# First attention of a four-layer megakernel: Wv and Wo folded per head, weights applied to the normalised tokens, context transposed by the host

## The reference

```
xn = layer_norm(x, gamma_x, beta_x)            # the 64 context tokens of ctx_1024
ln = layer_norm(latents, gamma_l, beta_l)      # the 64 tokens of x
q = ln @ Wq                                    # 8 heads of 64
k_x, v_x = split(xn @ Wkv);  k_l, v_l = split(ln @ Wkv)
k_x = rope_rotate_k(k_x)                       # halves swapped in each head, cos and sin
k = concat(k_x, k_l);  v = concat(v_x, v_l)    # 128 keys
out = softmax(q k^T / sqrt(64)) v  ->  (64, 512) @ Wo
x = x + tanh(g_xattn[0]) * out
```

## Time and profile before

| what | value |
|---|---|
| median of 3 runs | 2398.12 us (2397.97 to 2405.66) |
| the profiled execution, its own time | 2399.08 us |
| its span, first to last instruction | 2397.3 us |
| PE busy in the span | 87% |
| DVE, ACT, POOL busy | 79%, 51%, 14% |
| mean granted TensorE clock (of full) | 0.94 |
| first attention: first transfer to last x update | 36.4 to 695.5 us |

### The profile page before, as it was taken

The page is one execution under the profiler, slowest core; times in us unless marked ns, Lnnn a source line. Parts: engine busy times, 40 slices in busy tenths (PEclk is TensorE's granted clock), DMA queues, the critical chain, the costliest instruction groups (busy, mean ns, idle before and its releaser), DMA issues. The chain is left out here.

```text
span 2397.3 us, 51278 instructions
## 1 busy us (share of the span) xinstructions
PE 2076.7 (87%) x16365; PEld 1539.6 (64%) x16365; DVE 1888.4 (79%) x5125; ACT 1226.7 (51%) x2434; POOL 340.5 (14%) x680
## 2 busy tenths in 40 slices
PE   3999999999977888999998979699999987499507
PEld 3888888888853435777775757477777765244207
DVE  3899999999969898888885779566666668787785
ACT  1455555555533335677675646354544445307737
POOL 0111111111114443111111114100000022200000
PEclk9999999999988789999998989799999999699859
DMA  6111111111100000111110001112112111002442
GB/s 178 46 46 46 45 45 45 45 45 45 46 18 1 0 0 19 24 24 24 23 23 5 0 17 55 71 72 106 71 74 103 71 37 36 1 0 100 182 139 70
DMA packets 118317, 119.72 MB, mean 50 GB/s; under 512 B 45001, under 2 KB 101218, under 8 KB 116194
## 3 DMA queue, kind: packets, MB, share of 16 engines
q1 hardware_dynamic: 112248, 116.10, 16.0%
q10 hardware_dynamic: 5994, 2.70, 0.4%
HBM read 76.56 MB, written 25.43 MB: 43 GB/s over the span
## 5 line engine op out<-in xcount | busy, mean ns | idle before, releaser
L1658 DVE TENSOR_TENSOR arena<-arena 128x512 f32<-128x512 f32 (+1 forms) x256 | 171.1, 686 | 65.3 <-ACT arena L1696 59.7
L1696 ACT ACTIVATE arena<-banks,b1c 128x512 f32<-128x512 f32 x192 | 131.7, 687 | 168.4 <-PE banks L1571 168.2
L656 ACT ACTIVATE arena<-arena 128x512 f32<-128x512 f32 x128 | 80.8, 631 | 193.0 <-DVE arena L604 193.0
L888 PE MATMUL banks<-we,arena 128*128 128x512 f32 x256 | 141.5, 708 | 22.6 <-ACT arena L804 20.9
L1581 PEld LDWEIGHTS banks<-w2a,arena 128*128 128x128 f32 x1024 | 124.1, 192 | 28.7 <-issue 28.7
L217 DVE TENSOR_SCALAR xhat<-x_tiles,mean_var,rstd 128x128 f32 (+1 forms) x320 | 107.9, 374 | 33.6 <-POOL rstd L762 28.3
L1146 ACT ACTIVATE arena<-arena 128x512 f32<-128x512 f32 x128 | 80.7, 631 | 100.0 <-DVE arena L1098 100.0
L502 PE MATMUL banks<-arena 128*128 128x128 f32 x1024 | 131.3, 281 | 0.1
L1024 PE MATMUL banks<-arena 128*128 128x512 f32 x256 | 125.9, 615 | 3.9 <-ACT arena L1152 0.2
L1092 DVE TENSOR_REDUCE arena<-banks 128x8 f32<-128x512 f32 x128 | 87.7, 685 | 51.5 <-PE banks L1024 51.4
L518 PE MATMUL banks<-arena,wk 128*128 128x128 f32 x1024 | 126.6, 277 | 1.1 <-DVE arena L626 1.1
(11 more groups left out here) (271 smaller groups left out, 5402.1 us busy)
## 6 DMA issues: line engine op xcount, KB each, us to landing
arena<-coef_scratch SPq DMA_DIRECT2D x16, 2048.0 KB, 7.1
arena<-arena SPq DMA_DIRECT2D x128, 128.0 KB, 2.3
gated_scratch<-arena SPq DMA_DIRECT2D x16, 768.0 KB, 3.3
arena<-gated_scratch SPq DMA_DIRECT2D x16, 768.0 KB, 4.3
arena<-z1T_scratch SPq DMA_DIRECT2D x128, 64.0 KB, 2.2
arena<-ctxT_scratch SPq DMA_DIRECT2D x32, 256.0 KB, 2.8
arena<-in_ctx SPq DMA_DIRECT2D x64, 64.0 KB, 1.8
z1T_scratch<-arena SPq DMA_DIRECT2D x64, 64.0 KB, 1.5
```

The lines of the kernel that those rows point to most:

```text
L888: mm = pe.matmul(ps[:, 6 + t.par if h else 2 + j, :], xTg[g.par][:, j * P:(j + 1) * P], k.we0[:, 4 * h:4 * h + 4, :].rearrange("p e m -> p ...
L1658: dve.tensor_tensor(hT[g.par][rows, c, :], hT[g.par][rows, c, :], wide_coef[g.par][rows, e, :], ALU.mult).then_inc(s["scaled"].sem, 1)
L1696: act.activation(hT[g.par][:, c, :], ps[:, HID + c % NHID, :], ACT.Gelu, bias=k.b1c[:, c:c + 1])\
```

## The change

All in the first attention and what serves it:

- **Algebra.** The sum over keys is applied to the normalised tokens instead of the values: Y = zn^T probT gives, for each batch, 128 channels x (8 heads x 64 queries) in one matmul of 512 columns. `prepare` multiplies Wv of each head with Wo of that head (`wvo0`, 8 matmuls, two more ACT copies). The result is the sum over heads of Y times `wvo0`, 8 matmuls of 128x128. Values, the product with Wo, the `on` transposes and the column of ones go.
- **Softmax.** The maximum is no longer subtracted on DVE: it goes, negated and scaled by a small DVE operation (`nb`), as bias into the exponential, which reads PSUM directly, in four pieces of 128 columns for each batch. Row sums, reciprocal and scaling of the weights are DVE operations in SBUF, twice each (`normalise`).
- **Queries.** ACT copies them into the block diagonal `QBD`, zeroed once by POOL, instead of DVE's multiplication with a mask.
- **Keys.** Wq and Wk are loaded as they are (four copies on DVE go), so the swap of halves lies within each 64 rows: four transfers of 32 partitions instead of two of 64.
- **Context.** The host passes ctxT; one PE transpose, one ACT copy and one store for each tile go. Two transposes of the normalised tokens (`zn`) and one ACT copy come.
- **Order.** The x update runs two steps behind instead of one, the weight transposes one step later.

```diff
@@ sync
-                    sp.wait_ge(*f["xT_psum"](t.back(2)))
+                    sp.wait_ge(*s["zhat"](t.back(2)))
...
-                sp.wait_ge(*s["ctxT_sb"](t))
-                sp.dma_start(k.ctxT_dram[t.idx], cto[t.par]).then_inc(k.ctxT_stored.at(t), 16)
                 sp.wait_ge(*s["kc"](t))
                 if t.has(1):
                     sp.wait_ge(*s["ksin"](t.back(1)))
-                for to, of in ((slice(0, 64), slice(64, P)), (slice(64, P), slice(0, 64))):
-                    sp.dma_start(kr[to, :], kc[of, :]).then_inc(swapped.at(t), 16)
+                for n in range(4):
+                    to, of = n * 32, (n ^ 1) * 32
+                    sp.dma_start(kr[to:to + 32, :], kc[of:of + 32, :]).then_inc(swapped.at(t), 16)
@@ tensor
+                    pe.wait_ge(*s["pt_sb"](t, b + 1))
+                    pe.matmul(ps[:, PT + b, :], zn[t.par][:, b], probT[:, b], start=True, stop=True)\
+                        .then_inc(s["y_psum"].sem, 1)
...
+                for h in range(H0):
+                    mm = pe.matmul(ps[:, KC, 0:D], Y[:, h].rearrange("p b i -> p (b i)"), k.wvo0[:, h, :],
+                                   start=h == 0, stop=h == H0 - 1)
+                mm.then_inc(s["out_psum"].sem, 1)
@@ vector
+        def normalise(t, b):
+            dve.wait_ge(*s["prob"](t, (b + 1) * HPAIRS))
+            dve.tensor_reduce(ssum[:, b], prob[:, b], AX.X, ALU.add).then_inc(s["ssum"].sem, 1)
+            dve.wait_ge(*s["ssum"](t, b + 1))
+            dve.reciprocal(rec[:, b], ssum[:, b]).then_inc(s["srec"].sem, 1)
+            dve.wait_ge(*s["srec"](t, b + 1))
+            dve.tensor_tensor(prob[:, b], prob[:, b], rec[:, b].unsqueeze(2).broadcast_to([P, HPAIRS, P]), ALU.mult)\
+                .then_inc(s["normed"].sem, 1)
...
                 dve.wait_ge(*s["ksin"](t))
+                dve.wait_ge(*s["kcos"](t))
+                if t.has(1):
+                    dve.wait_ge(*s["s_psum"](t.back(1)))
@@ scalar
-                    act.wait_ge(*s["sshift"](t, b + 1))
-                    act.activation(prob[:, b], prob[:, b], ACT.Exp, scale=HD0 ** -0.5).then_inc(s["prob"].sem, 1)
-
+                    act.wait_ge(*s["nb"](t, b + 1))
+                    if t.has(1):
+                        act.wait_ge(*s["pt_psum"](t.back(1), b + 1))
+                    for c in range(HPAIRS):
+                        act.activation(prob[:, b, c], ps[:, S + b, c * P:(c + 1) * P], ACT.Exp, scale=HD0 ** -0.5,
+                                       bias=nb[:, b, c:c + 1]).then_inc(s["prob"].sem, 1)
```

More of the change, by code:

```diff
@@ L236, in prepare @@
     k.gates, k.spike_gate = sb("gates", [P, 8]), sb("spike_gate", [P, 1])
-    gates_raw, wq_raw, wk_raw = raw(8), raw(INNER), raw(INNER)
-    k.wq0, k.wk0, k.wv0 = (sb(n, [P, INNER]) for n in ("wq0", "wk0", "wv0"))
-    k.wo0 = sb("wo0", [P, HPAIRS, D])
+    gates_raw = raw(8)
+    k.wq0, k.wk0 = (sb(n, [P, INNER]) for n in ("wq0", "wk0"))
+    k.wvo0 = sb("wvo0", [P, H0, D])
+    wvT, wo_raw = (raw(INNER).rearrange("p (c d) -> p c d", c=HPAIRS) for _ in range(2))
     k.aff = sb("affine_columns", [P, 8])
@@ L350, in scalar @@
         act.activation(k.bout[:, :], ps[:, 7, D:2 * D], ACT.Copy, scale=k.gates[:, 2:3]).then_inc(folded_sb, 1)
+        act.wait_ge(folded, 3)
+        for n in range(2):
+            act.activation(k.wvo0[:, n::2, :], ps[:, n, :].rearrange("p (h d) -> p h d", d=D), ACT.Copy)\
+                .then_inc(turned_sb, 1)
     def vector(dve):
         all_loaded(dve)
[L356 to L360, removed]
         dve.tensor_scalar(bv_wide, k.konst[:, C_ONES:C_ONES + P], bcol[:, 0:1], None, ALU.mult).then_inc(built, 1)
@@ L492, in tensor @@
         k.ready(pe)
-        pe.wait_ge(preset, 2)
         def body(at):
+            if t := at(-1):
+                for b in range(PAIR):
+                    pe.wait_ge(*s["normed"](t, b + 1))
+                    if t.has(1):
+                        pe.wait_ge(*s["y_sb"](t.back(1), b + 1))
+                    for c in range(HPAIRS):
+                        mm = pe.transpose(ps[:, PT + b, c * P:(c + 1) * P], prob[:, b, c], k.ident)
+                    mm.then_inc(s["pt_psum"].sem, 1)
             if t := at(0):
@@ L504, in body @@
                     mm.then_inc(s["s_psum"].sem, 1)
[L505 to L511, removed]
+            if t := at(0):
+                if at(1):
+                    pe.wait_ge(*s["z_ready"](at(1)))
+                for b in range(PAIR):
+                    mm = pe.transpose(ps[:, TURN, (2 + b) * P:(3 + b) * P], Z[t.par][:, b].rearrange("p s i -> p (s i)"),
+                                      k.ident)
+                mm.then_inc(s["zn_psum"].sem, 1)
@@ L562, in body @@
[L562 to L572 removed]
+                elif t.has(1):
+                    pe.wait_ge(*f["x_updated"](t.back(1)))
```

242 lines of the change are left out of this document (114 added, 128 removed).

## The result

| what | before | after |
|---|---|---|
| median of 11 runs | 2398.71 us | 2410.85 us (2407.39 to 2414.34) |
| ratio after to before | | 1.0045, 95% interval 1.0036 to 1.0054 |
| profiled execution | 2399.08 us | 2409.06 us |
| its span | 2397.3 us | 2407.3 us |
| mean granted TensorE clock | 0.94 | 0.94 |

The changed kernel is slower by 0.45%, 12 us. That is inside the range given, 12.4 us above the forecast, and on the far side of the line between "no change" and "slower". The cause shows in the trace in the place that the prediction named; it is larger than the sum had it.

A forecast was written before the change was run, and what follows sets the result against it. Prediction: PE bounds the kernel at 10.03 us a step; after the change a DVE, ACT, SP, transfers ring takes 9.97. 63 steps give -3.8, preparation +2.9, filling +1.5: +0.6 us, stated as 2398.5 us, range 2374 to 2420.

The forecast's parts named there:

- no change: The forecast itself, chance 0.36: a step of 9.86 to 10.08 us, within 7.2 us of the kernel before.
- that ring: Steady step of the first attention: work passes DVE, ACT, SP, transfers and back to DVE once a step, 9.97 us.
- extra waits: On DVE, `nb` and L642 stand behind two and three waits instead of one: 0.07 us each, 0.14 a step.
- SP: four transfers: Issue of the key swap: the last of four starts 1.67 us after the first, 1.55 to 1.95.
- landing of 64 KB: Key swap transfer within SBUF, from issue to landing: taken as 1.85 us, between 1.5 and 2.3, plus 0.04 to DVE.
- slower rival: Key swap: landing stays at 2.3 us, step 10.42, time 2427 us; chance 0.29.
- ring through Y: Another circle, through ACT's copies of Y and PE's product with `wvo0`: 9.06 us, showing only if ACT were slower.
- Four pieces of exponential: ACT's exponential of the scores in 128-column pieces: 1.03 us by a trace row, against a page's 1.27.
- PE's new sum: PE's work in one step of the changed attention: 9.51 us, 0.52 less than before.
- faster rival: PE stays the bound as transfers land after 1.5 us, issued every 0.52: step 9.51, time 2370 us; chance 0.35.
- Preparation: Before the attention: 16 more PE instructions and two ACT copies, less removed DVE copies; +2.9 us, first transfer at 39.3.
- Filling and draining: First pass shows the two extra issues, and a tile's output part has one more stage: +1.5 us.

## Why the prediction came out as it did

The mechanism of the steady part was right. PE keeps up and doesn't set the step, DVE waits at L636 for the swap in each step, and the step is the sum of that ring. The time is inside the range, but 12 us above the forecast, and its 0.45% is what the prediction itself called slower: one step of the sum was sized too low. Term by term, the step of the timeline above:

| term | predicted | measured |
|---|---|---|
| DVE from L636 to the reduction | 3.42 | 3.35 |
| reduction and `nb`, to ACT | 0.93 | 1.01 |
| ACT: four pieces, `zn`, `kc`, to SP | 1.92 | 1.93 |
| three more issues, landing, to DVE | 1.67 + 1.89 = 3.56 | 306.74 - 302.87 = 3.87 |
| extra waits | 0.14 | 0, or inside the 1.01 |
| sum | 9.97 | 10.16 |

- **The step that failed is the size of "SP: four transfers" and "landing of 64 KB".** Four issues take 2.42 us, 0.605 each, so the last starts 1.82 after the first, not 1.67: the pair in the earlier trace rows hid that behind the first issue each further one takes about 0.6. The landing is 2.0 and not 1.85, so half the bytes brought back 0.3 of 2.3 us and not 0.45. With 0.05 left for the hand-over these are 0.31 us a step, nearly 20 us over the stage, of which other terms took back a part. My condition for the slower rival was issue and landing together over 3.63; they are 3.82. The rival's mechanism is what happened, at 10.18 instead of its 10.42, because the landing did not stay at 2.3. The rule cited there held in substance. The Trainium skill, "DMA: Bandwidth & Descriptors", section "Rules for kernel authors", advises against two transfers to disjoint halves of the partitions, as they share the same engines; here 32, 64 and 128 KB land in 2.0, 2.0 and 2.1 us in the experiments' traces, and the added issues are paid in full where they lie in the ring.
- **The extra waits** behind `nb` and L642 were priced at 0.07 each. From the reduction to `nb` pass 0.80 us in this step and 0.71 in the next, where 0.73 was the price without the wait; from L636 to L642 pass 0.73, where it was 0.72. So the first shows in every other step and the second not at all. This and the 0.07 that DVE is quicker took back part of the 0.31.
- **DVE's idle time** before L636 was forecast at 0.4 and is 0.8 (0.73 in the timeline). The 0.4 didn't follow from the prediction's own sums, which leave 9.97 - 9.29 = 0.68.
- **PE's idle time** was forecast before the scores (L513). It is there, but as much stands before L563, 0.3 us a step in the waits view, where PE waits for ACT's copy of Y. The prediction named this as a sign of the ring through Y, together with DVE never waiting at L636. DVE does wait there in all 64 steps, and the kernel with two transfers loses 0.47 us a step without a change in that ring, so it isn't the one that sets the step.
- **Four pieces of exponential** were priced by the row at 1.03 and took 1.01. By the section of the Trainium skill that the prediction cites ("ScalarE: Activation LUTs", "What ACT_TABLE_LOAD costs") four take 1.27 from start to end, an estimate; measured are 1.14, so here the trace decides. That they cost the step 0.4 is shown by the run with one piece.
- **PE's new sum**, 9.51, was 0.23 too high; with the ring cut, PE needs 9.28, and the step is 9.43. The forecast of the time doesn't use it, but the faster rival at 2370 does.
- **The faster rival** asked for issue and landing under 3.4 us and promised 2370. Even without any swap the step is 9.69 and the time 2375.61, since the x update at the head of DVE's order waits for PE's last product. I had not priced this second ring (DVE's update, gamma and beta, and reduction wait behind PE's L563). So it was not to be reached by the transfers alone.
- **Preparation**: +2.9 predicted, +0.4 measured (36.79 against 36.41 for the first context load). The terms as I wrote them add to 3.4, a slip of 0.5. What was wrong is the price of 16 instructions at 0.22 each, 3.5; they took 1.16. That much is chance: in three of the other traces with the same fold they took 2.08, and the load came at 38.0 to 38.3, +1.6 to +1.9. PE started 0.94 earlier (30.97 against 31.91), as the removed DVE copies led me to say, 0.8.
- **Filling and draining**: +1.5 predicted, +0.8 measured, but the 3.6 us of the first two steps belong here as well, and then it is +4.4. The prediction had put nothing for a lower clock while the pipeline fills. From the first load to the first L636 it is 0.7 less (50.5 - 36.8 against 50.8 - 36.4); from the last L636 to the end it is 1.5 more.

Together: 0.6 forecast; the time from the first L636 to the last adds 14.3 to it (10.5 + 3.8), 3.6 of them in the first two steps and the rest in the ring of the later ones; the preparation takes 2.5, the edges 0.7, the later stages 1.7. That makes the 10.0 us between the two profiled spans. The medians of 11 runs differ by 12.1. It is luck that the preparation and the later stages, which have nothing to do with the ring, went the other way by 4.2 us: this hides the 3.6 us of the first two steps, which the prediction didn't have.

## What to carry to other kernels

Add up not only each engine but each circle of work that closes from one step to the next; an edit that saves time on the fullest engine and puts two DMA issues into such a circle can lose. An issue or a copy costs nothing as long as the circle has slack and its whole price once it has none. So where a kernel gets a new order, look first at what stands between the wait and the transfer that others wait for: here the layout of the weights (two transfers instead of four) and the place of one small update were worth 2.0% between them. And before a slack is called used up, count the gaps of the engine behind it too. Last, don't take a mean step for the steady one: here two slow steps at the start made a third of the difference.

## What was not expected of the hardware

- Landing hardly depends on size for these transfers within SBUF: 2.0 us for 32 KB and 64 KB, 2.1 for 128 KB in the kernels with two transfers, 2.3 for 128 KB in the kernel before. The number of issues counts, about 0.6 us each when they follow one another.
- Matmuls of 64 rows that alternate between the two halves of the partitions run in part together: with instructions of 417 ns, 16 take 2.08 us in alternation and 3.09 when they keep to one half eight at a time. The Trainium skill, "TensorEngine Tiling (Array Packing)", section "Key Properties", says that different tiles of the array can load weights and multiply in parallel; this difference agrees. The 1.16 us of the kernel after have a second reason, instructions of 272 ns.
- With the long waits of the eight-transfer kernel the granted clock fell from 1.00 to 0.90 in the mean of the same stretch, and a step at the lower level took 13.51 us instead of 12.53. A wait in a ring can thus cost more than its length. The same wait of 2.5 us stood before a step that kept the full clock.
- While the pipeline fills, the changed kernel has a mean granted clock of 0.72 over 36 us and the kernel before 1.00, in the two profiled executions.
